# Self-attention inside a perceiver block: row-wise softmax with transposed probabilities, and a wider spread of its links over the steps

## What is computed

```python
x = x + xattn(layernorm(x), ctx, ctx)   # 8 x 64 queries, 1601 keys, width 256, 16 heads of 16, with biases
x = x + attn(layernorm(x))              # self-attention, causal, 64 x 64, 16 heads
x = x + ffn(layernorm(x))               # router softmax, best 2 of 8 experts, 256 -> 1024 -> 256, exact gelu
```

```python
q = q / math.sqrt(D)
scores = jnp.einsum('bhqd,bhkd->bhqk', q, k)
scores = jnp.where(causal[None, None], scores, jnp.float32(-jnp.inf))
attn = jax.nn.softmax(scores, axis=-1)
out = jnp.einsum('bhqk,bhkd->bhqd', attn, v)
```

## Time and profile before

| | us |
|---|---|
| median of 3 runs | 671.48 (670.67 to 673.57) |
| profiled execution, its own time | 674.92 |
| its span in the trace | 673.1 |
| PE busy | 647.2 (96%) |
| PE weight loads | 533.3 (79%) |
| DVE busy | 473.2 (70%) |
| ACT busy | 326.8 (49%) |
| POOL busy | 298.4 (44%) |
| DMA | 34.12 MB, mean 51 GB/s |

### The profile page before, as it was taken

The page is one execution under the profiler, slowest core; times in us unless marked ns, Lnnn a source line. Parts: engine busy times, 40 slices in busy tenths (PEclk is TensorE's granted clock), DMA queues, the critical chain, the costliest instruction groups (busy, mean ns, idle before and its releaser), DMA issues.

```text
span 673.1 us, 15769 instructions
## 1 busy us (share of the span) xinstructions
PE 647.2 (96%) x6408; PEld 533.3 (79%) x6408; DVE 473.2 (70%) x871; ACT 326.8 (49%) x533; POOL 298.4 (44%) x386
## 2 busy tenths in 40 slices
PE   7989999999999999999999999888999999999997
PEld 4778878778778868877886876657789999999997
DVE  4887767676759778476877864768778677667753
ACT  4355655654554554554455544345554444444431
POOL 2147787997766788596668757100000000000000
PEclk9999999999999999999999999878999999999999
DMA  5311110100110010110001000153003303320001
GB/s 177 135 50 50 39 39 26 51 26 25 27 50 2 26 52 25 26 51 25 27 25 26 1 2 1 33 220 127 1 1 126 115 12 125 125 98 26 0 0 33
DMA packets 13285, 34.12 MB, mean 51 GB/s; under 512 B 1563, under 2 KB 10532, under 8 KB 11044
## 3 DMA queue, kind: packets, MB, share of 16 engines
q1 hardware_dynamic: 13188, 33.19, 14.8%
q0 software_dynamic: 32, 0.01, 0.0%
HBM read 32.67 MB, written 0.52 MB: 49 GB/s over the span
## 4 chain that ended last, share of the span: by engine, by line
PE 79%; DVE 10%; issue 5%; POOL 3%; ACT 2%; DMA 0%; POOLq 0%; DVEq 0%; ACTq 0%
PE bank L1169 45%; PE bank L1363 9%; PE bank L1178 9%; PE bank L1349 4%; PE bank L1239 3%; POOL prob_sum L482 3%; PE bank L1282 2%; PE bank L1291 2%; DVE maxes L883 2%; DVE prob_sum L482 2%; DVE ctx_lo L466 1%; DVE shift L825 1%; ACT k_hi L618 1%; PE bank L1266 1%; DVE k_lo L864 1%
## 5 line engine op out<-in xcount | busy, mean ns | idle before, releaser
L482 POOL TENSOR_TENSOR prob_sum<-probs,prob_sum 128x256 f32<-128x256 f32 x336 | 268.5, 831 | 72.1 <-ACT probs L722 66.7
L722 ACT ACTIVATE probs<-bank 128x1024 f32<-128x1024 f32 (+1 forms) x104 | 106.7, 1026 | 115.3 <-PE bank L1363 103.2
L883 DVE TENSOR_REDUCE maxes<-bank 128x1 f32<-128x400 f32 (+1 forms) x256 | 129.5, 565 | 21.7 <-PE bank L1239 21.3
L704 ACT ACTIVATE h_raw<-bank,b_sb 128x512 f32<-128x512 f32 (+2 forms) x72 | 46.2, 642 | 107.0 <-PE bank L1169 106.9
L1169 PE MATMUL bank<-w_hi,h_hi 128*128 128x256 f32 x256 | 72.6, 284 | 0.0
L1169 PE MATMUL bank<-w_hi,h_lo 128*128 128x256 f32 x256 | 72.1, 282 | 0.0
L1169 PE MATMUL bank<-w_lo,h_hi 128*128 128x256 f32 x256 | 72.0, 281 | 0.0
L1178 PE MATMUL bank<-probs,v_sb 128*32 128x128 f32 (+1 forms) x1664 | 68.3, 283 | 2.5 <-DVE masked L815 2.0
L864 DVE SCALAR_TENSOR_TENSOR k_lo<-bank,bias_sb,k_hi 128x400 fp32r<-128x400 f32 (+2 forms) x64 | 40.4, 631 | 43.0 <-ACT k_hi L618 42.8
L1169 PE MATMUL bank<-wv_hi,ctx_hi 128*128 128x256 f32 (+1 forms) x208 | 65.4, 314 | 2.7 <-DVE maxes L883 2.4
L1363 PE MATMUL bank<-qbd_hi,k_hi 64*128 64x256 f32 (+1 forms) x416 | 67.9, 322 | 0.0
(11 more groups left out here) (158 smaller groups left out, 1422.0 us busy)
## 6 DMA issues: line engine op xcount, KB each, us to landing
raw<-in_w SPq DMA_DIRECT2D x16, 1024.0 KB, 6.8
ctx_raw<-in_ctx_t SPq DMA_DIRECT2D x16, 400.0 KB, 3.6
ctx_raw<-in_ctx_t SPq DMA_DIRECT2D x8, 402.0 KB, 3.6
ctx_raw<-in_ctx_t SPq DMA_DIRECT2D x8, 399.0 KB, 3.6
w_sb<-in_w_t SPq DMA_DIRECT2D x1, 1280.0 KB
w_raw<-in_w_t SPq DMA_DIRECT2D x2, 256.0 KB, 4.7
result<-x_all SPq DMA_DIRECT2D x4, 128.0 KB, 2.0
x_all<-in_x SPq DMA_DIRECT2D x1, 384.0 KB, 4.2
```

Source lines behind the costliest of these rows:

```text
L482: ins = engine.tensor_tensor(prob_sum[0:ROWS[k], cols], probs[0:ROWS[k], s % 2, cols], acc[0:ROWS[k]], ALU.add)
L704: nc.scalar.activation(h_raw[:, c % 2, 0:width], bank[:, at, 0:width], ACT.Gelu, bias=b1_sb[:, bass.ds(e, 1), c:c + 1].rearrange("p a b -> ...
L722: nc.scalar.activation(probs[0:ROWS[k], s % 2, :].rearrange("p (g n) -> p g n", g=G), bank[0:ROWS[k], score_bank(b, k):score_bank(b, k) + ...
L883: nc.vector.tensor_reduce(maxes[:, g * PAIRS + j, c:c + 1], src[:, 0:width], AX.X, ALU.max).then_inc(read_dve, 1)
```

## The change

The softmax of self-attention is now by rows. DVE adds the mask to the row scores, subtracts the row's maximum in place (`soft`, 128x512), ACT takes one exponential per batch a step later, DVE sums, inverts and multiplies a step after that, and PE transposes the finished probabilities (`t00` to `t11`), which ACT copies to `probs2`. Eight pieces of 128x64 per batch: in the first batch by `transpose`, in the second, whose result goes to partitions 64 to 127, by a fp32 matmul with the identity. Gone are the transposed scores with their two bf16 matmuls, the diagonal, the ones matmuls of `o0` and `o1`, and the division there. The queries of the second batch are spread one step after `s0`. The links lie over more steps in tile 3 and in the chain alone. In the last batch DVE reads the outputs of the batch before ahead of its sums, and each sum is taken one step later. Expert 0's gelu has its own table of steps, its chunks 5 to 7 move, and four splits of expert 1's weights are spread over four steps.

```diff
-CHAIN_AT = {3: ["y1"], 5: ["xt1"], 6: ["qk", "v"], 8: ["s0"], 10: ["st00", "st01"], 12: ["s1"], 13: ["st10", "st11"],
+CHAIN_AT = {3: ["y1"], 5: ["xt1"], 6: ["qk", "v"], 8: ["s0"], 10: ["s1"], 12: ["t00", "t01"], 14: ["t10", "t11"],
...
+CHAIN_AT_LAST = {2: ["y1"], 4: ["xt1"], 5: ["qk", "v"], 7: ["s0"], 9: ["s1"], 11: ["t00", "t01"],
+                 13: ["t10", "t11"], 15: ["o0", "o1"], 17: ["y2"], 19: ["xt2"], 20: ["router"], 23: ["gt"],
+                 24: ["b2"]}
...
+FIRST_HIDDEN = {0: [0, 1], 1: [2], 3: [3, 4], 6: [5], 7: [6], 9: [7]}
+FIRST_GELU = {0: [0, 1], 1: [2], 3: [3, 4], 8: [5, 6], 9: [7]}
...
+            def own_exponentials(units, s, t):
+
+                for kind in units.chain.get(s - 1, []):
+                    if kind in ("s0", "s1"):
+                        bi = int(kind[1])
+                        act.wait_ge(soft_ready, 2 * t + bi + 1)
+                        nc.scalar.activation(soft[:, bi], soft[:, bi], ACT.Exp).then_inc(soft_exp_done, 1)
...
+            def subtract_maxima(bi):
+                link(nc.vector.tensor_reduce(neg_max2[:, bi], soft[:, bi], AX.X, ALU.max, negate=True))
+                nc.vector.tensor_tensor(soft[:, bi], soft[:, bi], by_row(neg_max2[:, bi]), ALU.add).then_inc(soft_ready, 1)
+
+            def divide_rows(bi, count):
+
+                dve.wait_ge(soft_exp_done, count)
+                link(nc.vector.tensor_reduce(row_sums2[:, bi], soft[:, bi], AX.X, ALU.add))
+                link(nc.vector.reciprocal(row_sums2[:, bi], row_sums2[:, bi]))
+                nc.vector.tensor_tensor(soft[:, bi], soft[:, bi], by_row(row_sums2[:, bi]), ALU.mult).then_inc(rows2_ready, 1)
...
-                if "st01" in before and units is not TAIL:
-
-                    units.wait_read_act(dve, read_act, "st01")
+                if "s0" in before and units is not TAIL:
                     spread_own_queries(1, qbd2)
+                for kind in units.chain.get(s - 2, []):
+                    if kind in ("s0", "s1"):
+                        divide_rows(int(kind[1]), 2 * t + int(kind[1]) + 1)
...
-                    if more == bi == 1:
-                        sum_probabilities(nc.vector, dve, b, k, s, 1)
+                    if k == 1 and not is_first(b):
+
+                        dve.wait_ge(denom_done, b)
+                        at = (bi + 1) % 2 * Q
+                        own_heads(bank[:, O, :], o_read, b)
+                    if more == bi == 1 and k > 0:
+                        sum_probabilities(nc.vector, dve, b, k - 1, s - 1, 1)
...
+                    pe.wait_ge(rows2_ready, 2 * t + bi + 1)
+                    for j in range(PAIRS):
+                        turned, own_rows = dst[bi * Q:bi * Q + Q, j * P:j * P + P], soft[:, bi, g * PAIRS + j, :]
+                        if bi == 0:
+                            ins = nc.tensor.transpose(turned, own_rows, ident[:, :])
+                        else:
+                            ins = nc.tensor.matmul(turned, own_rows, ident[:, :], start=True, stop=True)
```

More of the change, by code:

```diff
@@ L124, in both_tiles @@
     return [("M", ROW_TILES * u + r) for u in pairs for r in range(ROW_TILES)]
-READ_BY_ACT = {"p1", "p2", "p3", "v", "V", "VL", "X", "xt1", "qk", "st00", "st01", "st10", "st11", "xt2", "router", "gt"}
+READ_BY_ACT = {"p1", "p2", "p3", "v", "V", "VL", "X", "xt1", "qk", "t00", "t01", "t10", "t11", "xt2", "router", "gt"}
 class Units:
@@ L172, in wait_read_act, with wait_read_dve @@
         eng.wait_ge(by_act, self.before[1] + self.counts(n + 1)[1])
+    def wait_read_dve(self, eng, by_dve, kind):
+        n = next(n for s in range(STEPS) for n, k, _ in self.at[s] if k == kind)
+        eng.wait_ge(by_dve, self.before[2] + self.counts(n + 1)[2])
     def wait_shift(self, eng, by_act, bi):
@@ L660, in step @@
                         unit(units, n, kind, u, t, b, parity)
+                own_exponentials(units, s, t)
             def prepare(k):
@@ L809, in normalize, with own_values, by_row @@
                                         ALU.mult).then_inc(done, 1)
+            def own_values(src, bi, read):
+                both = src[:, 0:G * P].rearrange("p (g s q) -> p g s q", g=G, s=2)
+                part = odd2[:, bi]
+                link(nc.vector.tensor_scalar(part, both[:, :, 1, :], mask_sb[:, HG + 1:HG + 2], None, ALU.mult))
+                nc.vector.scalar_tensor_tensor(out=o2_t[:, :, bi * Q:bi * Q + Q], in0=both[:, :, 0, :],
+                                               scalar=mask_sb[:, HG:HG + 1], in1=part, op0=ALU.mult, op1=ALU.add).then_inc(read, 1)
+            def by_row(values):
+                return values.unsqueeze(2).broadcast_to([P, G * PAIRS, Q])
+            def subtract_maxima(bi):
[6 more added lines that the diff above has]
+                nc.vector.tensor_tensor(soft[:, bi], soft[:, bi], by_row(row_sums2[:, bi]), ALU.mult).then_inc(rows2_ready, 1)
             def own_heads(src, read, count):
@@ L898, in unit @@
                 elif kind in ("s0", "s1"):
[L900 removed]
+                    nc.vector.tensor_tensor(soft[:, int(kind[1])], src.rearrange("p (n k) -> p n k", k=Q),
                                             causal_sb[:, :].unsqueeze(1).broadcast_to([P, G * PAIRS, Q]),
@@ L904, in unit @@
                     bi = int(kind[1])
-                    own_heads(src, read_dve, units.before[2] + units.counts(n + 1)[2])
-                    divide_heads(o2_t[:, :, bi * Q:bi * Q + Q], o2_ready)
+                    own_values(src, bi, read_dve)
                 elif kind == "b2":
@@ L925, in after_units @@
                     elif kind in ("s0", "s1"):
-                        link(nc.vector.tensor_reduce(neg_max2[:, :], masked[:, :, :], AX.X, ALU.max, negate=True))
-                        on_diagonal((shift2_alone if units is TAIL and kind == "s1" else shift2)[:, :, :],
-                                    neg_max2[:, :], shift2_ready)
+                        subtract_maxima(int(kind[1]))
             def route(units, t):
@@ L1078, in tile @@
                         split_w(0, SPLIT_W_AT.index(k), SPLIT_W_AT.index(k))
+                    if more == bi == 1 and k == KT - 1:
+                        sum_probabilities(nc.vector, dve, b, k, s, 1)
             tile(0, FIRST, 2, False)
@@ L1118, in _ @@
                     split_h(c, c, DONE_TILES * P, c >= 4)
-                if s == SECOND_LO_AT:
-                    for j in range(PIECES):
-                        split_w(1, 2 * PIECES + j, j)
+                if s in SECOND_LO_AT:
+                    split_w(1, 2 * PIECES + SECOND_LO_AT[s], SECOND_LO_AT[s])
             def last_rows():
@@ L1284, in unit @@
                                                    k2_t[:, g, bi * Q:bi * Q + Q], start=True, stop=True)
-                elif kind.startswith("st"):
-                    bi, g = int(kind[2]), int(kind[3])
-                    pe.wait_ge(shift2_ready, 2 * t + bi + 1)
-                    half = dst[bi * Q:bi * Q + Q, :]
-                    own_queries, shifts = (qbd2_alone, shift2_alone) if units is TAIL and bi else (qbd2, shift2)
-                    nc.tensor.matmul(half, k2_t[:, g, bi * Q:bi * Q + Q], own_queries[:, g].rearrange("p h q -> p (h q)"),
-                                     start=True, stop=False)
-                    nc.tensor.matmul(half, ones_bf[:, 0:Q],
-                                     shifts[:, g * PAIRS:(g + 1) * PAIRS].rearrange("p j c -> p (j c)"),
-                                     start=False, stop=False)
-                    ins = nc.tensor.matmul(half, causal_bf[:, :], ident_bf[:, :].unsqueeze(1).broadcast_to([P, PAIRS, P]),
-                                           start=False, stop=True)
+                elif kind[0] == "t":
+                    bi, g = int(kind[1]), int(kind[2])
+                    pe.wait_ge(rows2_ready, 2 * t + bi + 1)
[5 more added lines that the diff above has]
+                            ins = nc.tensor.matmul(turned, own_rows, ident[:, :], start=True, stop=True)
                 elif kind in ("o0", "o1"):
```

65 lines of the change are left out of this document (28 added, 37 removed).

## The result

| | before | after |
|---|---|---|
| median | 672.5 (670.7 to 674.7, 4 runs) | 662.0 (659.6 to 663.6, 4 runs) |
| profiled execution, its own time | 674.9 | 663.6 |
| its span in the trace | 673.1 | 661.7 |
| PE, DVE, ACT busy | 647.2, 473.2, 326.8 | 630.8, 475.3, 329.4 |

Ratio 0.984, 95% interval 0.981 to 0.987: faster by 1.6%, clear of no change: 10.5 us where 17.9 were forecast, and 1.5 us above the top of the range. PE's busy time fell by 16.4 us, the span by 11.4: part of what PE no longer does became waiting.

What follows compares the result with a forecast made beforehand. PE was taken to bound the middle tiles, with PE and DVE waiting for each other in the last batch. Gains 5.2 + 5.6 + 5.1 + 2.0 = 17.9 us took the median from 671.5 to 653.6 us, range 647.5 to 660.5.

Steps and rivals of the forecast that it cites:

- Removed and added work per chain, 4.1 us: PE in each of four chains: 6.56 us of scores and ones matmuls removed, 2.4 of turned pieces added, net 4.1 less.
- POOL's adds: Middle tiles: POOL's adds don't move in order, so they were put at nothing.
- PE ... stands 1.3 to 1.8 us; I take 1.5.: Middle tiles: PE waits ahead of `s1` for DVE's spread of the second queries, cutting each tile's gain to 2.6 us.
- The clock there still 1.00: Middle tiles: a sign to look for, PE's granted clock staying at 1.00 despite waits of some 1.5 us ahead of `s1`.
- rival 2: Middle tiles: the wait for the spread brings half clock, costing 6 us over two tiles, so 659.6 us; chance 0.10.
- Tile 3, 5.6 us: Tile 3 up to the last batch's step 14: net gain 5.6 us, bounds 3.5 and 6.5.
- For waits I leave 1.6.: Last batch: DVE's 27.5 us of work plus 1.6 of waits make 29.1 in place of 34.2, gaining 5.1.
- Rival 1: Last batch keeps its length: late sums hold ACT, PE idles, clock halves; 5.1 us not gained, 658.7 us; chance 0.12.
- The last chain, 2.0 us: Last chain: PE has 4.0 us less work, less waits of 0.8 and some 1.2; gain 2.0, bounds minus 1.0 and 4.0.
- Rival 3: All four chains: transposes are dear and count as idleness for the clock, costing 9 us, so 662.6 us; chance 0.04.
- Rival 5: Each chain: ACT, DVE and PE wait on each other in a ring, slower than before at 676.3 us; chance 0.03.

Runs made afterwards that it cites:

- e1: The changed kernel with the second batch's score unit `s1` one step later (11 instead of 10) in the middle tiles; median 659.2 us, 0.981 of the kernel before.
- a0: The changed kernel run again unedited, the run that experiments are compared with; median 662.8 us, 0.985 of the kernel before.
- e3: The changed kernel with expert 0's output 6 moved to step 11, behind `xt2`, with its splits; median 666.4 us, 0.991 of the kernel before.
- e6: The changed kernel with the last batch's final sum ahead of the eighth split of weights on DVE; median 661.2 us, 0.982 of the kernel before.
- e8: The changed kernel with `s1` a step later and the final sum ahead of the last split; median 658.7 us, 0.981 of the kernel before.
- e2: The changed kernel with DVE spreading the second queries ahead of step 9's maxima; median 660.8 us, 0.980 of the kernel before.
- e7: The changed kernel with all sixteen turned pieces made by fp32 matmuls, none by transpose; median 667.6 us, 0.992 of the kernel before.
- e9: e8 plus DVE subtracting each weight piece one step after ACT rounds it, the eighth behind the batch; median 656.5 us, 0.976 of the kernel before.
- e10: e9 plus `gt` and `b2` one step later each in the last chain; median 656.5 us, 0.980 of the kernel before.

## Why the prediction was wrong

- **Removed and added work per chain, 4.1 us.** Right in kind. Six-tenths of a microsecond for eight transposes was 0.82, 1.8 for eight matmuls 1.89; 0.3 us too little. e1's tiles, with the wait gone, are 3.2 us shorter than before, not 4.1. PE's busy time fell by 4.0 us, and its idle time rose by 0.8, from 2.2 us of 112 to 3.0 (108.90 less 105.88): 0.38 ahead of the denominators for POOL's sum, 0.2 by which the wait for the shift grew (1.62 to 1.83), and 0.16 ahead of the tile's other shift. POOL's adds I had put at nothing, since they keep their order; the shift's wait I had not looked at.
- **"PE ... stands 1.3 to 1.8 us; I take 1.5."** 1.77, at the top of the stated range: the subtraction took 1.10 and not 0.68 in tile 1, and in tile 2 it took 0.82 and the spread 1.70. e1 shows that this wait was a loss, as argued.
- **"The clock there still 1.00" was the step that failed in the middle tiles.** It fell in tile 1 and not in tile 2. I had it as rival 2 with 3 us per tile; in one tile it was 1.3. I weighed that wait against 1.99 and 0.62 us only the earlier trace rows; the 1.62 us for the shift in each middle tile, with the clock at 1.00, stood in the trace before and spoke against a rule by length. Terms for tile 2, the undisturbed one: 4.1 less 0.3 less 1.8 is 2.0, measured 1.8.
- **Tile 3, 5.6 us.** 6.1; right. Both output units moved out, and the wait for the diagonal went.
- **The last batch: "For waits I leave 1.6."** This step failed. DVE's work was 27.7 us where I had 27.5, which was right; its idle time was 4.5. 2.4 of that was for `w_hi`, which I had not costed, since a split had never waited while DVE was late itself (the earlier trace rows show 0.0 ahead of the splits). Once DVE is early it meets ACT's queue. How much of it comes varies: 1.0 us in a0, e1, e3, e6 and e8, whose batches take 30.3 to 30.8, but 1.8 in e2 and 2.1 in e7, whose batches take 31.7 and 31.9. In a0 DVE is idle for 3.2 us: besides the 1.0 for `w_hi`, 0.7 lies at the start until the denominators are done and 0.44 is for POOL's `rstd`. So the term for waits was 1.6 too small in a0 and 2.9 in the first execution. e9 takes the waits for `w_hi` away and the batch is 29.0 us long, against 29.1 forecast; but its eighth split stands behind the batch, and DVE's 26.2 us of work and 2.7 of idleness are not the 27.5 and 1.6 of the forecast, so that the agreement is partly luck. Rival 1 had the symptom (the batch keeps most of its length), but not through the sums. Half clock had no part in the length that shows: a0's batch, at a mean clock of 0.93, is as long as e1's at 1.00 (30.76 and 30.75), and e6's (30.36, 0.93) as e8's (30.34, 1.00).
- **The last chain, 2.0 us.** The waits came as told: 0.52 us ahead of the second batch's pieces (0.8 forecast) and 2.17 behind `y2` (1.65 forecast). The fall of the clock behind them was not in the sum, and that is the step that failed: e8 against e9 prices it at 2.4 us. I had taken from 1.99 and 0.62 us that only one long wait brings half clock; here three short ones were followed by it. In e9, where it stayed up, the piece is 2.1 us shorter than before. But the piece before was itself at 0.96, some 3.8 us at half clock, so that at the same clock the gain is probably smaller than the 2.0 forecast; no run shows by how much.
- **Rival 3** (dear transposes) is refuted by e7. The Trainium skill (TensorE: Matmul & The Clock Gate, Part 4, PE-mode transpose) gives about 275 ns for one, of 128x128 in bf16; the trace prints 273 ns as the mean duration of one of these, and in a row they cost 0.10 us each. By the row, the page's figure is a duration and not what a transpose holds PE for. Nor do the transposes bring half clock by themselves: e1's middle tiles, with eight of them each, stand at 1.00. **Rival 5**, the ring, didn't form in the middle tiles; the turn and turn about of DVE and ACT at `row_max`, `w_hi` and `w_lo` in the last batch is a small one of its kind.

In short: the work was read well from the profile before (DVE's in the last batch to 0.2 us, PE's in tile 3 to 0.5), and the shortfall of 6.5 us of span is mostly waits of up to two microseconds, many at places that had been covered by the lateness of the engine itself. Half clock made them larger in tile 1 and in the last chain, where PE is the bound or nearly, and not in the changed kernel's last batch, where DVE is.

## What to carry to other kernels

When a change makes the bound engine early, list what stands next in its queue and who produces it: those waits read 0.0 in the trace before and appear at once (here 2.4 us for `w_hi`). Put the consumer a step behind the producer. And price a new wait on PE twice, with and without the half clock that may follow, where PE sets the pace; several short ones close together can be followed by it as well (the changed kernel, e10), though they need not be (e9). Read the stage before with the same care: if the one trace at hand is of a long execution, part of what it shows as waste is not in the median.
